# Spreading the inverse softmax denominators by transfers instead of by a matmul, in a four-layer graph kernel

## The reference

```
L0: Q,K,V = x@W+b (8 heads of 32); w = exp(Q.K^T/sqrt(32) - max) * max(adj, 1e-8)
    x = layernorm((w / sum(w)) @ V @ Wo + bo + x)
L1: f = x@W+b; l = q(f) + k(f)^T + (1-adj)*-1e9; l = leaky(l)
    x = softmax(l) @ f + x
L2: Q,K,V as in L0; s = Q.K^T/sqrt(32) + a(x) + c(x)^T + log(adj + 1e-9)
    x = softmax(s) @ V + x
L3: as L1, with weights of its own
```

## Time and profile before

| what | value |
| --- | --- |
| three executions | 1797.73, 1798.22, 1798.81 us (median 1798.22) |
| profiled execution, its span | 1798.2 us, 68824 instructions |
| busy share PE, PEld, DVE, ACT, POOL | 98%, 92%, 82%, 76%, 41% |
| busy us PE, DVE, ACT, POOL | 1757.7, 1475.6, 1372.0, 731.3 |
| mean granted clock of TensorE | 0.995 |
| chain that ended last: PE, ACT, DMA, DVE | 87%, 3%, 3%, 3% |
| transfers: queue q1's share of 16 engines, mean rate | 12.1%, 41 GB/s |

### The profile page before, as it was taken

How to read it: one execution, slowest core, us unless ns; L and a number is a source line. 1 busy time by engine, 2 the same in 40 slices (tenths; PEclk the granted TensorE clock), 3 DMA queues, 4 the chain that set the end, 5 groups by cost and what they waited for, 6 DMA issues and landing times.

```text
span 1798.2 us, 68824 instructions
## 1 busy us (share of the span) xinstructions
PE 1757.7 (98%) x28155; PEld 1647.2 (92%) x28155; DVE 1475.6 (82%) x3361; ACT 1372.0 (76%) x3792; POOL 731.3 (41%) x797
## 2 busy tenths in 40 slices
PE   7999999999999999999999999999999999999997
PEld 6899999999999999999999999999999999999986
DVE  4688888888888888888888888888888888888875
ACT  3677787777787787787787787787787787787774
POOL 3343344343443343443443343343443443443421
PEclk8999999999999999999999999999999999999999
DMA  3101011011011011011011011011011011011100
GB/s 116 39 20 49 26 49 49 26 49 50 26 49 49 26 49 49 27 49 49 26 49 50 26 49 50 26 49 49 26 49 49 26 49 49 26 49 49 35 8 25
DMA packets 48261, 74.56 MB, mean 41 GB/s; under 512 B 5456, under 2 KB 21968, under 8 KB 47952
## 3 DMA queue, kind: packets, MB, share of 16 engines
q1 hardware_dynamic: 47376, 69.49, 12.1%
q10 hardware_dynamic: 576, 0.68, 0.1%
HBM read 53.37 MB, written 16.78 MB: 39 GB/s over the span
## 4 chain that ended last, share of the span: by engine, by line
PE 87%; ACT 3%; DMA 3%; DVE 3%; issue 2%; POOL 2%; SPq 0%; DVEq 0%; POOLq 0%; ACTq 0%
PE banks L1111 15%; PE banks L1176 14%; PE banks L1113 13%; PE banks L1112 13%; PE banks L1325 7%; PE banks L1220 6%; PE banks L1211 6%; DMA x_t<-x_t_dram 3%; PE banks L1199 2%; PE banks L1285 2%; PE banks L1225 2%; PE banks L1313 1%; PE banks L1319 1%; POOL weights_B L684 1%; PE banks L1279 1%
## 5 line engine op out<-in xcount | busy, mean ns | idle before, releaser
L684 POOL TENSOR_TENSOR weights_B<-weights_B,adj 128x512 f32<-128x512 f32 x64 | 113.0, 1766 | 299.1 <-ACT weights_B L765 299.1
L690 POOL TENSOR_TENSOR inv_parts_A<-inv_both_A,own 128x512 fp32r<-128x512 f32 x64 | 66.7, 1042 | 303.7 <-DVE inv_both_A L1035 303.7
L1000 DVE TENSOR_REDUCE least_cols_A<-banks 128x4 f32<-128x512 f32 x256 | 159.4, 684 | 33.8 <-PE banks L1176 33.7
L1000 DVE TENSOR_REDUCE least_B<-banks 128x4 f32<-128x512 f32 x256 | 172.6, 681 | 11.6 <-PE banks L1185 11.5
L1111 PE MATMUL banks<-w_hi_v,xt_hi 128*128 128x258 f32 (+1 forms) x512 | 157.3, 307 | 9.5 <-DVE pick L883 9.5
L1111 PE MATMUL banks<-w_hi_f,xt_hi 128*128 128x258 f32 x512 | 162.3, 317 | 2.3 <-DVE xt_lo L875 0.7
L839 ACT ACTIVATE fp<-banks 128x258 f32<-128x258 f32 x256 | 92.6, 390 | 89.1 <-PE banks L1113 89.1
L765 ACT ACTIVATE banks<-banks,v_B 128x256 f32<-128x256 f32 x384 | 153.4, 474 | 0.0
L1111 PE MATMUL banks<-xt_hi,w_hi_k 128*128 128x256 f32 x512 | 150.7, 294 | 0.3 <-DVE xt_lo L875 0.3
L1113 PE MATMUL banks<-w_lo_v,xt_hi 128*128 128x258 f32 (+1 forms) x512 | 145.1, 283 | 0.0
L1112 PE MATMUL banks<-w_hi_v,xt_lo 128*128 128x258 f32 (+1 forms) x512 | 145.0, 283 | 0.0
(11 more groups left out here) (192 smaller groups left out, 6172.0 us busy)
## 6 DMA issues: line engine op xcount, KB each, us to landing
x_t<-x_t_dram SPq DMA_DIRECT2D x64, 256.0 KB, 3.6
x_in<-x_dram SPq DMA_DIRECT2D x64, 256.0 KB, 3.6
out_dram<-x_out SPq DMA_DIRECT2D x64, 256.0 KB, 2.4
adj_t<-adj_t_dram SPq DMA_DIRECT2D x64, 128.0 KB, 3.4
adj<-adj_dram SPq DMA_DIRECT2D x64, 128.0 KB, 2.0
scratch<-weights_dram SPq DMA_DIRECT2D x9, 256.0 KB, 6.6
scratch<-weights_dram ACTq DMA_DIRECT2D x2, 256.0 KB, 4.3
out_bias<-L_gnn_bo_dram ACTq DMA_DIRECT2D x1, 128.0 KB, 7.8
```

The source lines that it names most:

```text
L684: pool.tensor_tensor(units, units, weight_of[where][:, G.four, :, :].unsqueeze(2).broadcast_to([P, GROUP, 2, P]), ALU.mult).then_inc(first ...
L1000: dve.tensor_reduce(to, bank[SCORE_BANKS[n]].rearrange("p (u m) -> p u m", u=UNITS), axis=AX.X, op=ALU.min).then_inc(maxed[where], 1)
```

## The change

The wide product, the copy of the heads, the rounding, the pair and POOL's pattern product are dropped, with their constants. `sums` is laid out so that a unit's denominators come in every fourth row; DVE writes the reciprocal to SBUF; SP issues four transfers (one per unit) that copy 32 rows of it to 128 partitions; and a new DVE step `scale` multiplies `use`'s bank with what has landed. `use`'s bank is held until then. Split and sum read the product from SBUF.

```diff
-                pool.memset(sums[:, u, u * part:(u + 1) * part], 1.0).then_inc(const_ready, 1)
+                pool.memset(sums[:, u, u:HEAD_DIM:UNITS], 1.0).then_inc(const_ready, 1)
...
+                elif name == "spread":
+                    sp.wait_ge(inverted[where], G.no + 1)
+                    G.wait_former(sp, ot_lo_ready if where == "A" else x3_ready, 1, 1)
+                    for u in range(UNITS):
+                        sp.dma_start(inv_wide[where][:, u, :],
+                                     inv[where][u:P:UNITS, :].unsqueeze(1).broadcast_to([HEAD_DIM, UNITS, P])
+                                     ).then_inc(inv_landed[where], 16)
...
-                        dve.reciprocal(bank[b][:, 0:P], bank[b][:, 0:P]).then_inc(inverted[where], 1)
-                        dve.wait_ge(inverted[where], G.no + 1)
-                        dve.tensor_copy(inv_hi[where][:, :], bank[b][:, 0:P]).then_inc(inv_rounded[where], 1)
...
+                        G.wait_former(dve, inv_landed[where], 16 * UNITS, 1)
+                        dve.reciprocal(inv[where][:, :], bank[b][:, 0:P]).then_inc(inverted[where], 1)
+                    elif name == "scale":
+                        dve.wait_ge(inv_landed[where], 16 * UNITS * (G.no + 1))
+                        dve.wait_ge(filled[BANK["use", where, 0]], fills.after(G, "use", where, 0))
+                        flat = inv_wide[where][:, :, :].rearrange("p u n -> p (u n)")
+                        dve.tensor_tensor(flat, bank[BANK["use", where, 0]], flat, ALU.mult).then_inc(ot_ready[where], 1)
```

```diff
+    "tensor": [
+        (4, "mask", "3", 0), (3, "turn_max", "B", 0), (3, "again", "B", 0), (3, "shift", "B", 0), (0, "q", "0", 0),
+        (0, "k", "0", 0), (1, "out_proj", "0", 0), (1, "out_proj", "0", 1), (2, "v", "2", 0), (0, "scores", "A", 0),
+        (3, "den", "B", 0), (2, "v", "2", 1), (2, "k", "2", 0), (1, "turn_x", "1", 0), (0, "turn_max", "A", 0),
+        (0, "again", "A", 0), (0, "shift", "A", 0), (3, "use", "B", 0), (2, "turn_rows", "2", 0), (1, "fc", "1", 0),
+        (1, "fc", "1", 1), (2, "q", "2", 0), (4, "turn_p", "3", 0), (1, "mask", "1", 0), (-1, "v", "0", 0),
+        (4, "mix", "3", 0), (0, "den", "A", 0), (2, "scores", "B", 0), (1, "turn_p", "1", 0), (3, "fc", "3", 0),
+        (3, "fc", "3", 1), (1, "mix", "1", 0), (0, "use", "A", 0)],
+    "vector": [
+        (0, "max", "A", 3), (3, "den", "B", 0), (1, "turn_x", "1", 0), (4, "inv", "3", 0), (0, "adj_t", "", 0),
+        (0, "weigh", "A", 1), (3, "scale", "B", 0), (0, "weigh", "A", 2), (1, "qk", "1", 0), (3, "sum", "2", 0),
+        (1, "mask", "1", 0), (0, "weigh", "A", 3), (1, "leak", "1", 0), (3, "turn_x", "3", 0), (1, "inv", "1", 0),
+        (0, "den", "A", 0), (4, "mix", "3", 0), (2, "max", "B", 0), (2, "max", "B", 1), (2, "max", "B", 2),
+        (2, "max", "B", 3), (3, "qk", "3", 0), (2, "max_parts", "B", 0), (1, "mix", "1", 0), (3, "mask", "3", 0),
+        (0, "scale", "A", 0), (3, "leak", "3", 0), (0, "split", "A", 0), (1, "turn_x", "2", 0), (2, "weigh", "B", 1),
...
+    "sync": [
+        (0, "load", "adj_t", 0), (0, "load", "x", 0), (7, "store", "", 0), (1, "spread", "A", 0),
+        (1, "load", "adj", 0), (-1, "load", "x_t", 0), (3, "spread", "B", 0)],
```

More of the change, by code:

```diff
@@ new lines @@
+    "vector": [
+        (0, "adj_t", "", 0), (0, "max", "A", 0), (0, "max", "A", 1), (0, "max", "A", 2), (0, "max", "A", 3),
+        (0, "weigh", "A", 1), (0, "weigh", "A", 2), (0, "weigh", "A", 3), (0, "den", "A", 0), (0, "scale", "A", 0),
+        (0, "split", "A", 0), (0, "out_proj", "0", 0), (0, "out_proj", "0", 1), (1, "max", "A", 0),
+        (1, "adj_t", "", 0), (0, "norm", "", 0), (1, "max", "A", 1), (1, "max", "A", 2), (1, "max", "A", 3),
[3 rows of a table added]
+        (1, "out_proj", "0", 1), (2, "max", "A", 0), (2, "adj_t", "", 0), (1, "norm", "", 0), (2, "max", "A", 1),
[3 rows of a table added]
+        (0, "max_parts", "B", 0), (1, "mix", "1", 0), (2, "scale", "A", 0), (3, "adj_t", "", 0),
+        (2, "split", "A", 0), (1, "turn_x", "2", 0), (0, "weigh", "B", 1), (2, "out_proj", "0", 0),
+        (0, "weigh", "B", 2), (0, "weigh", "B", 3), (2, "out_proj", "0", 1), (3, "max", "A", 0), (3, "max", "A", 1),
+        (2, "norm", "", 0), (3, "max", "A", 2), (0, "den", "B", 0), (3, "max", "A", 3), (2, "turn_x", "1", 0),
[6 rows of a table added]
+        (4, "max", "A", 0), (0, "inv", "3", 0), (4, "max", "A", 1), (3, "norm", "", 0), (4, "max", "A", 2),
[7 rows of a table added]
+        (5, "max", "A", 1), (1, "inv", "3", 0), (4, "norm", "", 0), (5, "max", "A", 2), (5, "max", "A", 3),
[7 rows of a table added]
+        (6, "max", "A", 1), (5, "norm", "", 0), (6, "max", "A", 2)],
@@ new lines @@
+    "sync": [
+        (0, "load", "x_t", 0), (0, "load", "x", 0), (0, "load", "adj", 0), (0, "load", "adj_t", 0),
+        (1, "load", "x_t", 0), (1, "load", "x", 0), (2, "load", "x_t", 0), (1, "load", "adj", 0),
+        (0, "spread", "A", 0), (1, "load", "adj_t", 0), (3, "load", "x_t", 0), (2, "load", "adj_t", 0),
+        (1, "spread", "A", 0), (2, "load", "adj", 0), (2, "load", "x", 0), (4, "load", "x_t", 0),
+        (3, "load", "adj_t", 0), (3, "load", "adj", 0), (3, "load", "x", 0), (2, "spread", "A", 0),
+        (4, "load", "adj_t", 0), (0, "spread", "B", 0), (3, "spread", "A", 0), (5, "load", "x_t", 0),
+        (4, "load", "x", 0), (1, "spread", "B", 0), (5, "load", "adj_t", 0), (6, "load", "x_t", 0),
+        (4, "load", "adj", 0), (4, "spread", "A", 0), (5, "load", "x", 0), (2, "spread", "B", 0)],
@@ L183 @@
     "tensor": [
[16 rows of a table removed]
[23 rows of a table added]
         (-1, "turn_max", "B", 0), (-2, "mask", "3", 0), (-1, "shift", "B", 0), (-1, "den", "B", 0),
[2 rows of a table removed]
[2 rows of a table added]
     "vector": [
[7 rows of a table removed]
-        (-3, "weigh", "B", 2), (-3, "weigh", "B", 3), (-1, "norm", "", 0), (-3, "den", "B", 0),
[11 rows of a table removed]
-    "scalar": [
[16 rows of a table removed]
+        (-2, "max", "A", 3), (-5, "den", "B", 0), (-6, "inv", "3", 0), (-3, "turn_x", "1", 0), (-2, "adj_t", "", 0),
[5 rows of a table added]
+        (-3, "turn_x", "2", 0), (-1, "adj_t", "", 0), (-4, "weigh", "B", 1), (-2, "out_proj", "0", 0),
+        (-4, "weigh", "B", 2), (-4, "weigh", "B", 3), (-2, "out_proj", "0", 1), (-5, "inv", "3", 0),
@@ new lines @@
+    "gpsimd": [
+        (-5, "weigh", "B", 0), (-2, "adj_t", "", 0), (-3, "rstd", "", 0), (-1, "turn_x", "0", 0),
+        (-6, "bias", "3", 0), (-1, "adj_t", "", 0), (-2, "weigh", "A", 0), (-5, "bias", "3", 0),
+        (-2, "penalty", "", 0), (-1, "penalty", "", 0), (-4, "weigh", "B", 0), (-1, "bias", "0", 0),
+        (-2, "rstd", "", 0), (-1, "weigh", "A", 0), (-3, "weigh", "B", 0), (-4, "bias", "3", 0), (-1, "rstd", "", 0),
+        (-3, "bias", "3", 0), (-2, "weigh", "B", 0), (-1, "weigh", "B", 0), (-2, "bias", "3", 0),
+        (-1, "bias", "3", 0)],
@@ new lines @@
+    "sync": [
+        (-2, "load", "adj_t", 0), (-2, "load", "x", 0), (-9, "store", "", 0), (-3, "load", "adj", 0),
+        (-8, "store", "", 0), (-3, "spread", "A", 0), (-1, "load", "x", 0), (-1, "load", "x_t", 0),
+        (-2, "load", "adj", 0), (-5, "spread", "B", 0), (-7, "store", "", 0), (-1, "load", "adj_t", 0),
+        (-6, "store", "", 0), (-2, "spread", "A", 0), (-1, "load", "adj", 0), (-4, "spread", "B", 0),
+        (-1, "spread", "A", 0), (-3, "spread", "B", 0), (-2, "spread", "B", 0), (-5, "store", "", 0),
+        (-4, "store", "", 0), (-3, "store", "", 0), (-1, "spread", "B", 0), (-2, "store", "", 0),
+        (-1, "store", "", 0)],
@@ L254 @@
 }
 ENGINES = ("tensor", "vector", "scalar", "gpsimd", "sync")
-FILL_NAMES = ("scores", "again", "turn_max", "use", "den", "wide", "turn_x", "k", "q", "v", "fc", "mask", "turn_p",
+FILL_NAMES = ("scores", "again", "turn_max", "use", "den", "turn_x", "k", "q", "v", "fc", "mask", "turn_p",
               "mix", "turn_rows", "out_proj")
@@ L533, in last_reader @@
             if name == "use":
-                return heads_ready[where], g + 1
+                return ot_ready[where], g + 1
             if name == "den":
-                return inv_split[where], g + 1
-            if name == "wide":
-                return (ot_lo_ready if where == "A" else x3_ready), g + 1
+                return inverted[where], g + 1
             if name == "v":
@@ L572, in load_weight, with step @@
                              ).then_inc(raw_landed[n], 16)
-            def step(name, G):
-                if name == "load":
+            def step(name, where, G):
+                if name == "load" and where == "x_t":
                     G.wait_former(sp, xt_ready["0"], 1, 1)
                     sp.dma_start(x_t[:, :], ins["x_t"][G.no]).then_inc(xt_landed, 16)
+                elif name == "load" and where == "adj_t":
                     G.wait_former(sp, adj0_ready, 1, 1)
@@ L580, in step @@
                     sp.dma_start(adj_t[:, :], ins["adj_t"][G.no]).then_inc(adj_t_landed, 16)
```

(32 more changed lines are left out.)

131 lines of the change are left out of this document (24 added, 107 removed), and 351 rows, old and new, of tables (EARLY, FILLERS, HOMES, LATE).

## The result

The changed kernel takes 1884.2 us (median of 1879.1 to 1889.3), the kernel before 1798.0: a ratio of 1.0486 with a 95% interval of 1.0464 to 1.0508. The forecast was 1791 us with a range up to 1808, so the change went the other way. The profiled execution took 1889.3 us (span 1887.5).

A forecast was written before the change was run, and what follows sets the result against it. The prediction took TensorE's stream, switches included, to bound the steady part. From 1798.2 us it summed -4 (stream), -10 and +2 (loads), +3 (head), +2 (drain) to 1791 us, range 1776 to 1808 for 8 in 10.

The forecast's parts named there:

- three signs of being wrong: Period over 27.0 us; VectorE's scale waiting mostly for the transfer, not use's bank; fill and drain growing over 10 us.
- Part 2: SyncE's loads: ordered singly, x_t no longer waits behind penalty, late norms go; -10 us (0 to -11), +2 for new stalls.
- +2 us: Allowance for rounds of the new order in which a transfer or POOL comes late.
- part 3: Spread of the reciprocal: lands in time off TensorE's path, 0 us, up to 0.8 a round if late; loads land easily.
- the first rival: Late spread: transfers land late or SyncE is held, so scale A comes late; 1810 to 1842 us, chance 0.19.
- Part 1: TensorE's stream: wide products leave, tiling switches join; -0.07 us a round, -4 us in all (-25 to +22).
- rival 2: TensorE's switches all cost alike, 0.2 us: +6 us instead of -4, time 1801; chance 0.18 together with rival 4 (change misses its place).
- Part 4: Head and tail: TensorE starts at about 17 us, +3 us (-1 to +8); drain +2 us (0 to +4).
- the 2 us given: Drain: the last group's two spreads each replace a chain of about 2.3 us by 3.7; +2 us (0 to +4).
- head term: Start: first adj_t issued behind eight weight loads, TensorE starts 7.5 us later, partly given back; +3 us (-1 to +8).

The follow-up runs named there:

- f2: Changed kernel with adj loaded first, scale A's product in PSUM, GpSimd's bias 3 before rstd, turn_x 0 after weigh A, VectorE's reciprocal B before two minima: 1794.1 us.
- e1: Changed kernel with only SyncE's order edited: a group's adj load issued first instead of behind spread A; 1848.3 us.
- e3: Changed kernel with only GpSimd's order edited: rstd behind bias 3 and turn_x 0 instead of ahead of them; 1855.2 us.
- b1: Kernel before the change, with only adj's load moved behind the next group's x_t instead of ahead of it; 1791.7 us, ratio 0.9968.
- f3: f2 without its reciprocal edit, layer B's spread issuing two of four transfers in groups 8 to 59 (half of B's division left out): 1793.3 us.
- g1: f2 with all four loads of the first group issued ahead of the eight weight loads, as in the kernel before; 1788.8 us.

## Why the prediction was wrong

**All three signs of being wrong came.** The period is 28.36 us; of VectorE's two scales, B waits for the transfer in 34 rounds of 49; fill and drain grew by 4.4 + 6.3 = 10.7 us. The first is nearly the whole loss.

**Part 2 is the step that failed**, in its last sentences: "I find the new order's waits met by about 0.4 to 1 us" and the +2 us for what is left. Against f2, which does the same work with them taken away, the stalls of the new order come to 28.36 - 26.72 = 1.64 us a steady round, and over the 63 rounds of the span to 1773.7 - (1706.5 - 28.1) = 95 us. No row of the prediction stands behind the 0.4 to 1 us: I had laid the steps of VectorE out with the lengths that the trace of before shows, and taken these for fixed. They hold only beside the GpSimd steps of that order. In the order of before GpSimd mostly lost: its weigh B takes 1.77 us on average against 1.30 for the same shape in layer A, and VectorE's xt_lo beside it 0.70. In the new one weigh B still comes second to ot_lo, but then VectorE comes second as well, three times a round. What brought GpSimd's steps to the first two is the adj load: part 3's "have most of a round to land" did not hold for it, as penalty and all that GpSimd has behind it stood waiting for adj (675.6 us of the span, 11.8 in the round shown), and with adj loaded first ot_lo was short again (e1); less met bias 3 by GpSimd's own order (e3). The rest of part 2 held in kind: the single loads took the old stalls away. In size, b1's timed gain is 5.8 us where -10 was forecast (the profiled executions' rounds, 27.00 and 26.85 us, would give 10 in 64 rounds).

**Part 3, the spread.** The landing behind an issue came as taken: the page gives 2.0 us for both layers. The issues did not:

```profile
inv_wide_A<-inv_A SPq DMA_DIRECT2D x256, 64.0 KB, 2.0
inv_wide_B<-inv_B SPq DMA_DIRECT2D x256, 64.0 KB, 2.0
```

```profile
921.13 2.48 SPq L622 DMA_DIRECT2D inv_wide_B<-inv_B  x4
```

Four take 2.48 us here, 0.62 each, and up to 3.83 us in other rounds, where the earlier trace rows gave 0.44 for one. (A round has 13 issues, four loads, a store and eight copies, and not the 15 of part 3.) And for layer B I counted the time from den B's end as if VectorE took the reciprocal at once. In after's round den B ends on TensorE at about 917 and the reciprocal starts at 920.16, behind minima and less. In the changed kernel itself scale waited for a transfer only 24 us in 40 waits, nearly all of them of scale B:

```profile
DVE inv_wide_B L1038 <- DMA inv_wide_B<-inv_B: 21.9, 34, 1.4
```

So the first rival alone was not the loss; it became the bound when the collisions were gone, and f3 and f2 show that 15 us hang on it then. Its place, scale A, was wrong: it is scale B that waits, and mask 1 behind it.

**Part 1.** Compared with b1, both without stalls, f2's round is 26.85 - 26.72 = 0.13 us shorter; -0.07 was forecast. That it comes so near is in part luck, as my prices were not those of the trace. Five rows of after's timeline of TensorE, two column blocks with what follows them:

```profile
901.19 1.08 PE L1216 MATMUL banks<-weights_A,sums 128*32 128x128 f32 x32
902.20 1.17 PE L1172 MATMUL banks<-kt_B,qt_B 32*128 32x128 f32 x32
...
921.89 0.66 PE L1195 MATMUL banks<-least_rows_A,minus_pick 4*128 4x128 f32 x16
922.48 1.08 PE L1207 MATMUL banks<-weights_B,v_B 128*32 128x128 f32 x32
923.49 0.33 PE L1319 MATMUL banks<-ident,c_cols 128*128 128x128 f32 x1
```

A column block takes 1.01 us to its successor whether that is a row block or a transpose, 0.11 over the 0.90 to another column block, and shift A goes over into use B after 0.59 us where it took 0.69 to fc. Shift B, in the same round, reaches a full matmul after 0.59 us too (908.66 to 909.25). The prediction's rule from the Trainium skill, "TensorEngine Tiling (Array Packing)", Key Properties, says that a change of mode drains the engine; the trace agrees that leaving a column block costs something whatever follows, but not that all changes cost alike, as rival 2 had it: the same change, from shift to full matmuls, took 0.69 us in one place and 0.59 in another. The +6 us of that rival did not come; which of the prices made the difference, no run here separates.

**Part 4.** TensorE's first matmul came at 16.2 us (17 forecast), and g1 shows what that costs: 1794.1 to 1788.8, 5 us (3 forecast). The drain lengthened more than the 2 us given: from the last group's transpose to the end of the span it is 79.7 us before and 1791.3 - 1706.5 = 84.8 in f2, by its tile over the whole span:

```profile
L1267 PE MATMUL banks<-ident,least_cols_A x64: 272/273/454, 28.1 to 1706.5; 128*128 128x128 f32 x64
```

Which part of these 5 us is the longer spread and which the late order was not tried.

With the stalls away, the sum of the prediction is nearly met, in part because its errors go both ways: f2 lies at 1794.1 and g1, without the head term, at 1788.8, with 1791 forecast. The other terms held within 5 us each; the one that was set small without a row behind it, +2 us, made the 95 us.

## What to carry to other kernels

When an order is moved, check every VectorE step with both inputs in SBUF against what GpSimd does at that time: here the later of the two waited for the other's end (VectorE's 128 x 512 steps ended 0.55 us behind it), and the lengths in a trace already contain who came second. Then look what waits for the step: in b1 less comes second in 42 of 53 rounds, at 0.56 us, and TensorE loses nothing. A stall that is removed shows the next one (here the spread's landing), so edits that help alone can hurt together until the chain behind them is followed. A transfer put between two engines costs the issues of all its parts and the place of its source in the issuing engine's order, and everything ordered behind its wait (here adj) moves with it.

## What the hardware showed that was not expected

A VectorE step on 2 elements per row took 0.99 us beside a GpSimd step of 1.04 us, and 0.18 (mean of the kernel before) without. SyncE needed about 0.6 us for the issue of a copy within SBUF of 64 KB in 512-byte rows (four in 2.48), 0.43 for most loads of 256 KB. And the same 128 x 512 step on GpSimd takes 1.30 us when it comes first and about 1.7 us beside VectorE's splits, in every kernel here.
